# Queries and keys of latent attention projected once a batch, their rows copied into head tiles by DMA

## What is computed

```python
k_eff = (W_dq.T @ W_uq.T @ W_uk).reshape(nh, hs, n_kvl)
v_eff = jnp.transpose((W_uv.T @ W_o.T).reshape(n_kvl, nh, hs), (1, 0, 2))
c_kv = x @ W_dkv.T
q = (x @ W_dq.T @ W_uq.T).reshape(B, T, nh, hs)
q_lat = jnp.einsum('bqhd,hdl->bhql', q, k_eff)
attn = jnp.einsum('bhql,bkl->bhqk', q_lat, c_kv) / sqrt(hs)
attn = jax.nn.softmax(jnp.where(causal, attn, -jnp.inf), axis=-1)
y_lat = jnp.einsum('bhqk,bkl->bhql', attn, c_kv)
y = jnp.einsum('bhql,hld->bqhd', y_lat, v_eff).reshape(B, T, C)
```

## Time and profile before

| | us |
|---|---|
| median of three runs | 2139.76 |
| the profiled execution, its own time | 2146.62 |
| its span, first to last instruction | 2144.8 |
| latent attention in it, L1060 to the last L1395 | 874 to 1322.9 |
| TensorE busy over the span | 81% |
| VectorE, GpSimd, ScalarE busy | 64%, 46%, 44% |
| mean granted TensorE clock | 0.945 |

### The profile page before, as it was taken

The page is one execution under the profiler, slowest core; times in us unless marked ns, Lnnn a source line. Parts: engine busy times, 40 slices in busy tenths (PEclk is TensorE's granted clock), DMA queues, the critical chain, the costliest instruction groups (busy, mean ns, idle before and its releaser), DMA issues. The chain is left out here.

```text
span 2144.8 us, 48275 instructions
## 1 busy us (share of the span) xinstructions
PE 1746.9 (81%) x19914; PEld 1024.5 (48%) x19914; DVE 1369.1 (64%) x2002; ACT 938.8 (44%) x1503; POOL 979.3 (46%) x692
## 2 busy tenths in 40 slices
PE   1578888888888887799999997678888888888885
PEld 1345444545545544455555553344444555555543
DVE  2466777666776664456666654577777776666752
ACT  1134444544445443245555554234444544544532
POOL 2444455455455451444444441445445545445530
PEclk9888999999999999589999998799999999999998
DMA  4333343455343452000000000243444534355441
GB/s 143 37 58 63 68 73 64 74 77 86 63 78 63 79 75 50 12 1 2 1 2 1 1 1 1 37 73 63 64 77 73 86 65 76 63 85 86 85 78 36
DMA packets 66060, 118.94 MB, mean 55 GB/s; under 512 B 13183, under 2 KB 23603, under 8 KB 63667
## 3 DMA queue, kind: packets, MB, share of 16 engines
q1 hardware_dynamic: 65843, 115.85, 32.1%
HBM read 49.61 MB, written 3.28 MB: 25 GB/s over the span
## 5 line engine op out<-in xcount | busy, mean ns | idle before, releaser
L953 POOL TENSOR_TENSOR QK<-QK,RB 128x1024 f32<-128x1024 f32 x128 | 302.2, 2361 | 120.2 <-DMA RB<-RN 120.2
L793 DVE SCALAR_TENSOR_TENSOR TP<-banks,cols,tab 128x1024 f32<-128x1024 f32 x256 | 318.3, 1274 | 52.5 <-PE banks L457 46.5
L947 POOL TENSOR_TENSOR QK<-TP 128x512 f32<-128x512 f32 x128 | 164.7, 1287 | 332.0 <-DVE TP L793 288.8
L1315 DVE TENSOR_REDUCE NM<-banks 128x2 f32<-128x1024 f32 (+3 forms) x256 | 202.9, 820 | 129.4 <-PE banks L1128 129.4
L1244 ACT ACTIVATE PTL<-banks 128x1024 f32<-128x1024 f32 (+1 forms) x192 | 168.1, 884 | 192.9 <-PE banks L1159 190.5
L816 DVE TRANSPOSE_TENSOR_REDUCE MX<-banks 128x16 f32<-128x512 f32 x256 | 160.2, 682 | 122.3 <-PE banks L494 122.3
L649 ACT ACTIVATE SQ<-banks 128x512 f32<-128x512 f32 x128 | 76.6, 599 | 279.1 <-PE banks L457 278.8
L834 DVE TENSOR_TENSOR OT<-banks,OT 128x512 f32<-128x512 f32 x128 | 85.3, 687 | 158.6 <-DMA OT<-sums_d 143.9
L939 POOL TENSOR_TENSOR HTL<-Z,HTH 128x512 fp32r<-128x512 f32 x32 | 37.8, 1182 | 303.8 <-ACT HTH L643 303.8
L457 PE MATMUL banks<-HTH,wqkv_h 128*128 128x512 f32 x256 | 125.3, 490 | 54.4 <-DVE TP L793 43.2
L655 ACT ACTIVATE SQ<-banks 128x512 f32<-128x512 f32 x128 | 76.7, 599 | 200.3 <-DVE TP L793 200.3
(11 more groups left out here) (182 smaller groups left out, 3636.0 us busy)
## 6 DMA issues: line engine op xcount, KB each, us to landing
RB<-RN SPq DMA_DIRECT2D x512, 64.0 KB, 4.0
OT<-sums_d SPq DMA_DIRECT2D x128, 256.0 KB, 4.0
V<-V SPq DMA_DIRECT2D x32, 512.0 KB, 6.0
V<-V SPq DMA_DIRECT2D x32, 384.0 KB, 7.1
RB<-vars_d SPq DMA_DIRECT2D x32, 256.0 KB, 3.3
X<-in_L_attn_x SPq DMA_DIRECT2D x8, 256.0 KB, 4.5
out<-X SPq DMA_DIRECT2D x8, 256.0 KB, 4.6
wqkv_raw<-in_L_ffn_wqkv SPq DMA_DIRECT2D x1, 1536.0 KB
```

Source lines behind the costliest of these rows:

```text
L793: nc.vector.scalar_tensor_tensor(out=TP[:, o:o + 2, :], in0=BK[4 + z][:, :].unsqueeze(1).to_broadcast([P, 2, T]), scalar=q, in1=tab[:, e, ...
L947: nc.gpsimd.tensor_tensor(QK[:, m, 0, :], TP[:, 2, :], TP[:, 1, :], ALU.subtract)
L953: nc.gpsimd.tensor_tensor(QK[:, m, :, :], QK[:, m, :, :], RB[:, m, :].unsqueeze(1).to_broadcast([P, 2, T]), ALU.mult).then_inc(S["nr_ok"], 1)
L1315: last = nc.vector.tensor_reduce(NM[:, G % 2, i, 24 + 32 * h0:57 + 32 * h0:32], PAIR[at(m) % RING][:, :, o:o + (i + 1) * P], AX_X, ALU.max ...
```

## The change

The folded weights are kept once, 128 x 128 for queries and for keys. `queries(b)` and `keys(b)` run once a batch and give all 16 heads' 128 channels, three matmuls each. ScalarE rounds the result to `HIGH` straight from the bank, VectorE subtracts it from the bank into `LOW`. Then SP issues, for each group, 12 DMAs into QS (four heads, three row blocks of 8 partitions x 512) and 12 into KS, with one semaphore for each slot of a ring; `scores` and `add_max` wait on these. The rows that no DMA writes are set once: KS filled from the column `one_row`, QS zeroed, on VectorE ahead of the first `xt`. GpSimd's `stack_q` and `stack_k` go. The batch's own work moves: statistics to r = 0 to 3 of the batch's first group, the normalisation to steps (0,5), (1,0), (1,1), transposes to (1,2), projections to (1,4) and (1,5), values to (2,0); (g, r) is group and step for the next batch. GpSimd's loop goes by steps. In the constants two columns go.

```diff
-                (Wq_s[:, :, 0:3, :], stacked(BK[4]), float(DG) ** -0.5),
+                (fold[:, 0, :], BK[4][:, 0:P], float(DG) ** -0.5),
                 (ve[:, :], BK[5][0:QL, 0:P], 1.0), (keT[:, :], BK[6][0:QL, 0:P], 1.0),
-                (Wv_s[:, :], BK[0][:, 0:P], 1.0), (Wk_s[:, :, 0:3, :], stacked(BK[1]), 1.0)]):
+                (fold[:, 2, :], BK[0][:, 0:P], 1.0), (fold[:, 1, :], BK[1][:, 0:P], 1.0)]):
...
-    AHEAD, QRING, KRING = 2, 3, 4
-    C_AT, Q_AT, K_AT = 1, 2, 4
-    XT_AT, XL_AT, V_AT, VL_AT = (AHEAD, 0), (AHEAD, 1), (AHEAD, 5), (AHEAD + 1, 0)
+    QRING, KRING = 3, 4
+    C_AT = 1
+    XT_AT, XL_AT, Q_AT, K_AT, V_AT = (1, 2), (1, 3), (1, 4), (1, 5), (2, 0)
+    QL_AT, KL_AT, VL_AT = (1, 5), (2, 0), (2, 1)
...
-    RAW = sb("RAW", [P, 2, T])
-    HI = sb("HI", [P, 2, T])
+    HIGH = sb("HIGH", [P, 2, 2, T])
+    LOW = sb("LOW", [P, 2, 2, T])
...
+            def rows(dst, G, n, arrived, terms):
+                b, g = divmod(G, GROUPS)
+                for r, src in enumerate(terms):
+                    for h in range(LG):
+                        head = (g * LG + h) * DG
+                        sp.dma_start(dst[32 * h + r * DG:32 * h + (r + 1) * DG, G % n, :],
+                                     src[head:head + DG, b % 2, :]).then_inc(arrived[G % n], 16)
+
+            sp.wait_ge(S["rows_ok"], 1)
+            for G in range(ALLG):
+                sp.wait_ge(S["ql_ok"], G // GROUPS + 1)
+                if G >= QRING:
+                    sp.wait_ge(S["qc_ok"], G - QRING + 1)
+                rows(QS, G, QRING, qs_in, (HIGH[:, 0, :, :], HIGH[:, 0, :, :], LOW[:, 0, :, :]))
+                sp.wait_ge(S["kl_ok"], G // GROUPS + 1)
+                if G >= KRING:
+                    sp.wait_ge(S["t_in"], UN * (G - KRING + 1))
+                rows(KS, G, KRING, ks_in, (HIGH[:, 1, :, :], LOW[:, 1, :, :], HIGH[:, 1, :, :]))
...
-            def project(G, s):
-                b, g = divmod(G, GROUPS)
+            def project(b, s, ready):
+                pe.wait_ge(S["xl_ok"], b + 1)
+                if b == 0:
+                    pe.wait_ge(S["fl_ok"], 1)
+                claim(B_PREP, ready, b + 1)
...
-                    last = nc.tensor.matmul(BK[B_PREP][:, :], w[:, s, g, :].bitcast(F32R),
+                    last = nc.tensor.matmul(BK[B_PREP][:, :], w[:, s, :].bitcast(F32R),
...
-            def queries(G):
-                pe.wait_ge(S["xl_ok"], G // GROUPS + 1)
-                if G == 0:
-                    pe.wait_ge(S["fl_ok"], 1)
-                claim(B_PREP, "rq_ok", G + 1)
-                project(G, 0).then_inc(S["q_in"], 1)
-
-            def keys(G):
-                claim(B_PREP, "rk_ok", G + 1)
-                project(G, 1).then_inc(S["k_in"], 1)
+            def queries(b):
+                project(b, 0, "ql_ok").then_inc(S["q_in"], 1)
+
+            def keys(b):
+                project(b, 1, "kl_ok").then_inc(S["k_in"], 1)
...
-                    pe.wait_ge(S["qs_ok"], G + 1)
-                    pe.wait_ge(S["ks_ok"], G + 1)
+                    pe.wait_ge(qs_in[G % QRING], 16 * 3 * LG * (G // QRING + 1))
+                    pe.wait_ge(ks_in[G % KRING], 16 * 3 * LG * (G // KRING + 1))
...
+                if batch_at(m, Q_AT):
+                    queries(batch_at(m, Q_AT))
+                if batch_at(m, K_AT):
+                    keys(batch_at(m, K_AT))
                 if batch_at(m, V_AT):
                     values(batch_at(m, V_AT))
-                if r == Q_AT and G + AHEAD < ALLG:
-                    queries(G + AHEAD)
-                if r == K_AT and G + AHEAD < ALLG:
-                    keys(G + AHEAD)
...
-            def raw_q(G):
-                act.wait_ge(S["q_in"], G + 1)
-                if G >= 1:
-                    act.wait_ge(S["qs_ok"], G)
-                nc.scalar.activation(RAW[:, 0, :], BK[B_PREP][:, :], ACT.Copy).then_inc(S["rq_ok"], 1)
-
-            def raw_k(G):
-                act.wait_ge(S["k_in"], G + 1)
-                if G >= 1:
-                    act.wait_ge(S["ks_ok"], G)
-                nc.scalar.activation(RAW[:, 1, :], BK[B_PREP][:, :], ACT.Identity,
-                                     bias=one_row).then_inc(S["rk_ok"], 1)
+            def high_q(b):
+                act.wait_ge(S["q_in"], b + 1)
+                if b >= 2:
+                    act.wait_ge(qs_in[(GROUPS * (b - 1) - 1) % QRING],
+                                16 * 3 * LG * ((GROUPS * (b - 1) - 1) // QRING + 1))
+                nc.scalar.activation(HIGH[:, 0, b % 2, :].bitcast(F32R), BK[B_PREP][:, :],
+                                     ACT.Copy).then_inc(S["qh_ok"], 1)
+
+            def high_k(b):
+                act.wait_ge(S["k_in"], b + 1)
+                nc.scalar.activation(HIGH[:, 1, b % 2, :].bitcast(F32R), BK[B_PREP][:, :],
+                                     ACT.Copy).then_inc(S["kh_ok"], 1)
...
+            def low_rows(b, s, high, low):
+                dve.wait_ge(S[high], b + 1)
+                nc.vector.tensor_tensor(LOW[:, s, b % 2, :].bitcast(F32R), BK[B_PREP][:, :],
+                                        HIGH[:, s, b % 2, :], ALU.subtract).then_inc(S[low], 1)
...
-                dve.wait_ge(S["qs_ok"], G + 1)
+                dve.wait_ge(qs_in[G % QRING], 16 * 3 * LG * (G // QRING + 1))
...
+            nc.vector.tensor_copy(KS[:, :, :].bitcast(F32R), one_row.unsqueeze(2).to_broadcast([P, KRING, T]))
+            nc.vector.memset(QS[:, :, :], 0.0).then_inc(S["rows_ok"], 1)
             xt(0)
             low_x(0)
+            low_rows(0, 0, "qh_ok", "ql_ok")
+            low_rows(0, 1, "kh_ok", "kl_ok")
...
-                if b < NB and G % GROUPS == 0 and r >= UN - NT:
-                    norm_stats(dve, S, b * NT + r - (UN - NT))
+                if b < NB and G % GROUPS == 0 and r < NT:
+                    norm_stats(dve, S, b * NT + r)
+                if b < NB and (G % GROUPS, r) in ((0, 5), (1, 0), (1, 1)):
+                    t = ((0, 5), (1, 0), (1, 1)).index((G % GROUPS, r))
+                    if t == 0 and b >= 2:
+                        dve.wait_ge(S["xt_in"], b - 1)
+                    for tt in ((0, 1), (2,), (3,))[t]:
+                        norm_apply(dve, S, b * NT + tt, U[:, b % 2, tt, :])
                 g = group_at(m, Y_LAG)
                 if g is not None:
                     result(g)
-                if b < NB and G % GROUPS == 1 and r >= UN - NT:
-                    if r == UN - NT and b >= 2:
-                        dve.wait_ge(S["xt_in"], b - 1)
-                    norm_apply(dve, S, b * NT + r - (UN - NT), U[:, b % 2, r - (UN - NT), :])
                 if batch_at(m, XL_AT):
                     low_x(batch_at(m, XL_AT))
+                if batch_at(m, QL_AT):
+                    low_rows(batch_at(m, QL_AT), 0, "qh_ok", "ql_ok")
+                if batch_at(m, KL_AT):
+                    low_rows(batch_at(m, KL_AT), 1, "kh_ok", "kl_ok")
...
-            def stack_q(G):
-                pool.wait_ge(S["rq_ok"], G + 1)
-                link(nc.gpsimd.tensor_scalar(HI[:, 0, :].bitcast(F32R), RAW[:, 0, :], low_q, None, ALU.mult))
-                if G >= QRING:
-                    pool.wait_ge(S["qc_ok"], G - QRING + 1)
-                nc.gpsimd.tensor_tensor(QS[:, G % QRING, :].bitcast(F32R), RAW[:, 0, :], HI[:, 0, :],
-                                        ALU.subtract).then_inc(S["qs_ok"], 1)
-
-            def stack_k(G):
-                pool.wait_ge(S["rk_ok"], G + 1)
-                link(nc.gpsimd.tensor_scalar(HI[:, 1, :].bitcast(F32R), RAW[:, 1, :], low_k, None, ALU.mult))
-                if G >= KRING:
-                    pool.wait_ge(S["t_in"], UN * (G - KRING + 1))
-                nc.gpsimd.tensor_tensor(KS[:, G % KRING, :].bitcast(F32R), RAW[:, 1, :], HI[:, 1, :],
-                                        ALU.subtract).then_inc(S["ks_ok"], 1)
...
-            for n in range(ALLG + 2):
-                if n % GROUPS == 1 and n // GROUPS + 1 < NB:
-                    norm_rstd(pool, S, n // GROUPS + 1)
-                if n + AHEAD < ALLG:
-                    stack_q(n + AHEAD)
-                    stack_k(n + AHEAD)
-                if 0 <= n - 2 < ALLG:
-                    add_result(n - 2)
+            nc.gpsimd.memset(VL[:, :, :, :, DG:DG + 1], 1.0)
+            nc.gpsimd.memset(VL[:, :, :, :, DG + 1:32], 0.0).then_inc(S["preset"], 1)
+            for m in range(STEPS):
+                G, r = divmod(m, UN)
+                if r == 4 and G % GROUPS == 0 and G // GROUPS + 1 < NB:
+                    norm_rstd(pool, S, G // GROUPS + 1)
+                g = group_at(m, Y_LAG)
+                if g is not None:
+                    add_result(g)
```

More of the change, by code:

```diff
@@ L49, in shape_constants @@
     causal = np.where(np.arange(P)[None, :] <= np.arange(P)[:, None], 0.0, BIG).astype(np.float32)
-    part = row % 32 // DG
-    split = [part == 2, part == 1, row % 32 == 24]
+    one = [row % 32 == 24]
     hsum = row // 32 == np.arange(32)[None, :] // 8
@@ L120, in macaron @@
```

(25 more changed lines are left out.)

63 lines of the change are left out of this document (20 added, 43 removed).

## The result

| | before | after |
|---|---|---|
| median, us | 2140.34 (2129.42 to 2142.68) | 2263.92 (2261.42 to 2267.33) |
| ratio, with 95% interval | | 1.059 (1.055 to 1.063) |
| span of the profiled execution | 2144.8 | 2265.5 |
| latent attention in it | 448.9 | 577.6 |
| mean granted TensorE clock | 0.945 | 0.895 |

Some executions of this program run a few per cent slower with nothing changed; the medians and ratios given are those of the others. The change costs 123.6 us where I had forecast 62. In the profiled executions the spans differ by 120.7: latent attention is 128.7 longer (862.62 to 1440.22 against 873.97 to 1322.85), the stages ahead of it are 11.3 shorter, which is no more than before's own runs differ among themselves, and the last stage is 3.3 longer. So the whole loss lies in the stage that was changed.

A forecast was written before the change was run, and what follows sets the result against it. SP's issue rate was to replace TensorE's instruction order as the bound of latent attention: 768 x 0.61 - 405.1 gives +63.4 us, setup -1, so 2139.8 + 62.4 = 2202 us; range 2118 to 2270.

The forecast's parts named there:

- One issue: Latent attention, SP's queue: each of 768 SBUF-to-SBUF DMAs was taken to occupy SP for 0.61 us (between 0.578 and 0.632).
- SP's holds: Latent attention, between SP's issues: SP's four waits a group were costed at 3 us in all (0 to 5).
- The tail: Latent attention's end: from group 31's first scores to the stage's end, 25.0 us as in the kernel before.
- third rival, C: Latent attention: TensorE's granted clock falls to 0.82 and batch groups delay SP; +23 over the forecast, 2225 us; chance 0.12.
- The start: Latent attention's start: VectorE's fill of KS and zeroing of QS add 2.7 us; the queries' low part stands at 887.3.
- Bank waits: Latent attention: TensorE's keys and values wait for the low parts, 2.5 us a batch, at most 4.6, hidden under SP's wait.
- first rival, A: Latent attention: SP's issue is cheap (at most 0.45 us) and TensorE stays the bound; 2122 us; chance 0.20.
- B: SP's queue in latent attention: a DMA of few rows costs extra, 0.84 us each; +240, 2379 us; chance 0.12.
- The signs I had named: Latent attention: QC steady 14.6 us apart, TensorE busy about 75% from 922 on, SP without idle time; feed-forward times kept.

## Why the prediction came out short

The mechanism was the forecast one: SP issues 768 DMAs in order, TensorE waits at a group's first scores, and its saved projections buy nothing. Three experiments that touch only SP's time (20 or 28 issues, a cheaper source) move the kernel by that time, or by as much of it as lies above TensorE's path. The sizes were off, all but one of them in one direction. The stage in the profiled execution was to take 512.2 us (13.3 to `ql_ok`, 768 x 0.61, 3 for the waits, 2.4 landing, 25.0 to the end) and took 577.6:

| term | forecast | measured | difference |
|---|---|---|---|
| stage start to SP's first issue | 13.3 | 15.8 | +2.5 |
| 768 issues | 468.5 | 512.3 | +43.8 |
| SP held or stretched between them | 3 | 13.5 | +10.5 |
| landing after the last issue | 2.4 | 1.4 | -1.0 |
| last group's first scores to the end | 25.0 | 34.6 | +9.6 |

**One issue, 0.667 and not 0.61.** This is the step that failed, two thirds of the miss. I interpolated between sums_d<-DR (0.536, 4 rows) and RB<-RN (0.624, 32 rows), as if the cost grew with rows. The number stood in the trace: 512 SBUF-to-SBUF issues at a median of 0.624, a gap of 0.04. I wrote it down (0.666, +105) and then used it only for the upper part of my range. The measured 2264 does lie inside that range, near its end of 2270, but by luck: the end stood for 0.70 an issue, and what came to it was 0.667 and some 22 us from the other terms. The most frequent row of the same kind is a better estimate than a line between two forms.

**SP's holds.** The timeline has one gap of 0.10 instead of 0.04 at nearly each of the 63 later starts of a half group, 3.5 us and so what I had costed for the waits. The rest is what I had at nothing. The gate on QC held SP twice (SP's waits in the stage):

```profile
SPq L1064 <- DVE QC L1333: 2.6, 2, 1.9
SPq L1057 <- DVE LOW L1311: 1.1, 2, 0.6
```

and eight issues took 0.72 to 1.66 us instead of 0.62, 5.7 us in all, spread over the stage, with no cause that the trace names. RB<-RN had shown a maximum of 1.731; with 768 in a row such outliers are on the path.

**The tail.** From group 31's first scores on TensorE is alone again, and I took before's 25.0 us. But it enters this stretch after a wait of 3.05 us:

```profile
1405.66 0.37 PE L1126 MATMUL banks<-causalb,identb 128*128 128x128 bf16 x2 [3.05 <-issue]
...
1439.77 0.45 POOL L1389 TENSOR_TENSOR X<-X,Y 128x128 f32<-128x128 f32 x1 [5.21 <-DVE Y L1342]
```

and is granted 0.60 from 1405 to 1435. With the filling matmuls it is granted 1.00, and the same work takes 24.9 us: so the 9.6 are the clock. A stretch copied from a kernel that never waits is too short for one that does. My third rival had 5 us for this and only as part of itself.

**The start.** The two fills took 1.21 and 1.34 us, 2.55 together, against my 2.7. What I hadn't seen is another instruction on VectorE:

```profile
865.69 4.92 DVE L300 TENSOR_SCALAR U<-X,mv,rstd 128x128 f32<-128x128 f32 x4 [1.13 <-POOL rstd L296]
870.53 1.21 DVE L1350 CAST KS<-cst 128x2048 fp32r<-128x2048 f32 x1
872.01 1.34 DVE L1351 MEMSET QS<- 128x1536 f32 x1 [0.27 <-issue]
```

The same four normalisations took 1.11 before. XTL thus ends 12.7 us after the stage's start and not 10.1; from there to the queries' LOW are 3.08 us, as I had it (3.15).

**Bank waits.** Seven batches of 2.5 us were the guess; 28.0 us of them on `banks` stand in the changed kernel's waits:

```profile
PE banks L1092 <- DVE LOW L1311: 17.0, 7, 2.4
PE banks L1103 <- DVE LOW L1311: 11.0, 6, 2.0
```

That is 4.3 a batch, and 5.0 with XTL's, at and above my upper end. I had looked at a wait that 64 quiet copies of ScalarE had left at 1.4 at most; now two engines in series stand between the projection and the bank's release, and each has queued work ahead. Here SP hides most of it, but in a kernel without that bound it decides. The first rival had the stage 17 us shorter than before's; with six DMAs it was 9.1 longer, 26 us off. Seven batches at 54.6 in place of 50.2, waits and lower clock together, are 31; its first scores came 5 us earlier than that rival had them.

**The rivals.** *A* had the wrong price of an issue, and with the issues gone it was still 26 us off in the stage. *B* (0.84 an issue) is out as sized; a form of few rows is dearer by 0.03, not 0.2. *C*, that TensorE loses its clock, did happen (0.76 from 940 to 1340) and cost little where SP is late anyway: a late TensorE can reach SP only through the gates of the rings, and those held it 2.6 us in the whole stage. In the tail it is the 9.6. I had sized it by a mean of 0.82, 12.8 us for a plain group and so under SP's pace. But the clock has two levels, and at the lower one a plain group takes 17.4, over SP's 16.0: that the rings covered this was luck of their depth, and with 20 issues they no longer did.

**The signs I had named.** QC did not come evenly at 14.6: the groups of a batch took 10.5 to 26, since the ring of three lets SP run ahead and the batch group uses that up. The average would have told; one distance would not. TensorE's busy share was 86%, not 75%: at half the clock the same work keeps it busy longer. The feed-forward stages kept their times, within the 11 us that before's own runs differ.

## What to carry to other kernels

Count the DMAs that one queue must issue for each unit of work, times the median issue of that very kind in a trace (here 0.667 us with its gap between two SBUF addresses), before counting bytes; the rate of a queue becomes the kernel's as soon as it is over the pace of the busiest engine. Then lay the data out so that one DMA fills a term of all tiles: an interleaved order of rows turned 24 DMAs into six and gave the same products. When a projection's bank is released through two engines in series, put the next user of that bank several steps later: that was worth 33 us here, and 29 more when the rest was spaced out and GpSimd's fills were moved. And when a faster queue gives less than its issues say, look at TensorE's granted clock stretch by stretch, not at its mean.
